# Attention and mixture-of-experts layer on one core: head 0's query rows on another DMA queue

## The reference

```python
xn = _layernorm(x)                                   # (1, 4096, 256)
q = (xn @ Wq.T); k = (xn @ Wk.T); v = (xn @ Wv.T)    # 16 heads of 16
energy = einsum('bqhd,bkhd->bhqk', q, k)
attn = softmax(energy / sqrt(256), axis=-1)
out = einsum('bhqk,bkhd->bqhd', attn, v)
scores = softmax(xf @ gate_w.T); idx = top_k(scores + gate_b, 2)
y = sum over the 2 chosen experts of weight * (silu((xf@w1+b1)*(xf@w3+b3)) @ w2 + b2)
z = the same expert form with the shared weights
return x + out + y + z
```

## Time and profile before

| | |
|---|---|
| median of 3 runs | 2168.85 us (2167.26 to 2175.11) |
| span of the profiled execution | 2166.9 us |
| PE busy | 2141.9 us, 99% |
| ACT busy | 2019.5 us, 93% |
| DVE busy | 814.3 us, 38% |
| POOL busy | 243.2 us, 11% |
| chain that ended last | PE 91%, ACT 7%, DVE 1% |

### The profile page before, as it was taken

How to read it: one execution, slowest core, us unless ns; L and a number is a source line. 1 busy time by engine, 2 the same in 40 slices (tenths; PEclk the granted TensorE clock), 3 DMA queues, 4 the chain that set the end, 5 groups by cost and what they waited for, 6 DMA issues and landing times.

```text
span 2166.9 us, 38385 instructions
## 1 busy us (share of the span) xinstructions
PE 2141.9 (99%) x15772; PEld 977.0 (45%) x15772; DVE 814.3 (38%) x1541; ACT 2019.5 (93%) x2229; POOL 243.2 (11%) x242
## 2 busy tenths in 40 slices
PE   8899999999999999999999999999999999999998
PEld 5732344444444444444444444444444444444322
DVE  7531234334434434434334334334334434544200
ACT  6599999999999999999999999999999999999998
POOL 0102665200000000000000000000000002223200
PEclk9999999999999999999999999999999999999999
DMA  8661434222222213213222322213213222332120
GB/s 286 241 226 47 133 107 132 75 63 66 74 66 68 78 51 83 77 51 85 63 62 71 79 62 73 79 49 85 71 55 85 63 74 72 104 99 64 57 79 3
DMA packets 225758, 187.27 MB, mean 86 GB/s; under 512 B 112407, under 2 KB 194926, under 8 KB 225582
## 3 DMA queue, kind: packets, MB, share of 16 engines
q1 hardware_dynamic: 212702, 149.35, 24.1%
q0 software_dynamic: 11824, 35.40, 5.1%
q10 hardware_dynamic: 1056, 0.07, 0.0%
HBM read 130.21 MB, written 54.53 MB: 85 GB/s over the span
## 4 chain that ended last, share of the span: by engine, by line
PE 91%; ACT 7%; DVE 1%; DMA 0%; issue 0%; SPq 0%; DVEq 0%; ACTq 0%
PE PS L842 41%; PE PS L829 29%; PE PS L854 12%; ACT probs L1112 6%; PE PS L865 6%; PE PS L664 0%; PE PS L665 0%; PE PS L668 0%; DMA qk_parts<-probs 0%; DVE probs L1248 0%; DVE stats L1224 0%; PE PS L640 0%; ACT x_parts L997 0%; ACT x_full L998 0%; PE PS L731 0%
## 5 line engine op out<-in xcount | busy, mean ns | idle before, releaser
L1112 ACT ACTIVATE probs<-PS 128x1024 f32<-128x1024 f32 x2048 | 1920.0, 1081 | 94.9 <-PE PS L829 80.1
L842 PE MATMUL PS<-probs,v_head 128*32 128x512 f32 x8192 | 1001.1, 601 | 1.0 <-ACT probs L1112 0.8
L829 PE MATMUL PS<-q_ring,k_stack 50*128 50x512 f32 x4096 | 741.3, 446 | 5.2 <-ACT probs L1112 3.5
L829 PEld LDWEIGHTS PS<-q_ring,k_stack 50*128 50x128 f32 x4096 | 332.8, 185 | 623.5 <-ACT probs L1112 564.2
L842 PEld LDWEIGHTS PS<-probs,v_head 128*32 128x32 f32 x8192 | 206.6, 108 | 447.2 <-issue 361.2
L1508 DVE TENSOR_SCALAR gate_in<-PS,bias_sb 128x256 f32<-128x256 f32 x165 | 79.6, 482 | 754.5 <-PE PS L854 735.7
L854 PE MATMUL PS<-x_hi,w_hi 128*128 128x256 f32 (+1 forms) x660 | 201.6, 305 | 0.0
L854 PE MATMUL PS<-x_hi,w_lo 128*128 128x256 f32 (+1 forms) x660 | 186.5, 283 | 0.0
L854 PE MATMUL PS<-x_lo,w_hi 128*128 128x256 f32 (+1 forms) x660 | 185.5, 281 | 0.0
L1172 POOL DMA_DIRECT2D slot_y<-y_sb x39 | 27.8, 714 | 1320.7 <-DVE y_sb L1576 1287.1
L854 PEld LDWEIGHTS PS<-x_hi,w_hi 128*128 128x128 f32 (+1 forms) x660 | 118.6, 180 | 60.1 <-issue 60.1
(11 more groups left out here) (166 smaller groups left out, 1194.4 us busy)
## 6 DMA issues: line engine op xcount, KB each, us to landing
w_raw<-in_w SPq DMA_DIRECT2D x110, 352.0 KB
k_stack<-qk_parts SPq DMA_DIRECT2D x120, 128.0 KB
w_raw<-in_w SPq DMA_DIRECT2D x55, 256.0 KB
q_ring<-qk_parts SPq DMA_DIRECT2D x384, 32.0 KB
slot_x<-part_a SPq DMA_DIRECT2D x39, 256.0 KB, 2.3
slot_in<-slot_x SPq DMA_DIRECT2D x156, 64.0 KB, 2.4
slot_y<-y_sb POOLq DMA_DIRECT2D x39, 256.0 KB, 2.6
qk_parts<-part_a SPq DMA_DIRECT2D x18, 512.0 KB, 4.0
```

The source lines that it names most:

```text
L829: last = pe.matmul(bank(2 * score_buffer(turn, g) + r), k_stack[rows, kt * P:(kt + 1) * P], q_ring[rows, sweep, i * QC:(i + 1) * QC], star ...
L842: last = pe.matmul(bank(O_BANK)[VW * j:VW * (j + 1), :], v_head[:, kt, :], probs[:, slot, (j % 2) * QC:(j % 2 + 1) * QC], start=(kt == 0), ...
L1112: nc.scalar.activation(probs[:, prob_slot(g), :], bank(2 * score_buffer(h, g), 2), ACT.Exp, scale=ENERGY_SCALE).then_inc(s_exp, 1)
```

## The change

Six edits:

- `load_q_rows`, `load_q_shift` and `store_shift` take the queue as an argument. Head 0's first sweep (12 row loads, the store of the shift's first half, 4 shift loads) is issued by GpSimd, on a semaphore of its own, `s_qfirst`. SP goes from key chunk 6 straight to query chunk 4. The shift's second half stays on SP, behind chunk 7.
- Query chunks 4 to 7 each get a store semaphore (`s_qlate`). `keep_values(12)` waits for chunk 4's alone.
- Query chunk 6 stands in `key_part[1]` instead of `probs`; ACT therefore waits for the store of key chunk 7 before it splits chunk 6.
- The shift's semaphore becomes two, one for each half.
- GpSimd's memset of `w2_raw` and of `zeros` stand behind its new DMAs, with waits for chunks 5 and 6. DVE's router waits for chunks 6 and 7.
- ACT gets one exponential of one element, behind the last square root.

```diff
-        query_part = [in_values, in_stage, in_values, in_stage, in_values, in_stage, in_xn, key_part[0]]
+        query_part = [in_values, in_stage, in_values, in_stage, in_values, in_stage, key_part[1], key_part[0]]
@@ store_queries
-                    sp.dma_start(store_v[s][:, 0:DT, c * QC:(c + 1) * QC], query_part[c][:, s, :, :].bitcast(f32)).then_inc(s_qst[c % 2], 16)
+                    landed = s_qst[c % 2] if c < FIRST else s_qlate[c - FIRST]
+                    sp.dma_start(store_v[s][:, 0:DT, c * QC:(c + 1) * QC], query_part[c][:, s, :, :].bitcast(f32)).then_inc(landed, 16)
@@ SP
-            for half in range(2):
-                sp.wait_ge(s_qst[half], stored(FIRST - 2 + half))
-            load_q_rows(0, 0)
             store_queries(4)
             store_queries(5)
             sp.wait_ge(s_kst[(NCH - 1) % 2], stored(NCH - 1))
             load_k_chunk(NCH - 1)
-            store_shift(0)
             store_queries(6)
             store_queries(7)
-            sp.wait_ge(s_sst, 16 * NP_)
-            load_q_shift(0, 0, s_q[0])
+            store_shift(sp, 1)
             sp.wait_ge(s_flag, 1)
             flag = sp.value_load(flag_i[0:1, 0:1], min_val=0, max_val=1)
-            store_shift(1)
-            for half in range(2):
-                sp.wait_ge(s_qst[half], stored(NCH - 2 + half))
+            for c in range(FIRST, NCH):
+                sp.wait_ge(s_qlate[c - FIRST], 16 * NP_)
@@ PE, scores
-                    pe.wait_ge(s_q[sweep], h * HEAD_Q + HEAD_Q)
+                    if h == 0 and sweep == 0:
+                        pe.wait_ge(s_qfirst, HEAD_Q)
+                    else:
+                        pe.wait_ge(s_q[sweep], (h + sweep) * HEAD_Q)
@@ ACT
                 if i == 0 and c == 6:
-                    act.wait_ge(s_tr, NCH)
+                    act.wait_ge(s_kst[1], stored(7))
                 if n == 12:
-                    act.wait_ge(s_qst[0], stored(6))
+                    act.wait_ge(s_qlate[0], 16 * NP_)
             nc.scalar.activation(qnorm[HALF:P, :], bank(5)[HALF:P, :], ACT.Sqrt).then_inc(s_qn, 1)
+            nc.scalar.activation(rec[0:1, 0:1], ident_sb[0:1, 0:1], ACT.Exp)
@@ POOL
-            pool.wait_ge(s_kst[1], stored(NCH - 1))
-            pool.wait_ge(s_qst[1], stored(NCH - 1))
+            for half in range(2):
+                pool.wait_ge(s_qst[half], stored(FIRST - 2 + half))
+            load_q_rows(nc.gpsimd, 0, 0, s_qfirst)
+            store_shift(nc.gpsimd, 0)
+            pool.wait_ge(s_sst[0], 16 * NP_)
+            load_q_shift(nc.gpsimd, 0, 0, s_qfirst)
+            pool.wait_ge(s_qlate[1], 16 * NP_)
             nc.gpsimd.memset(w2_raw[FT[2]:P, 2, :], 0.0).then_inc(s_wz, 1)
             pool.wait_ge(s_wz, 1)
             pool.wait_ge(s_v, NT // 2)
+            pool.wait_ge(s_qlate[2], 16 * NP_)
             nc.gpsimd.memset(zeros, 0.0).then_inc(s_zero, 1)
```

More of the change, by code:

```diff
@@ L271, in layer_program @@
         s_qst = [sem("s_qst0"), sem("s_qst1")]
+        s_qlate = [sem(f"s_qlate{i}") for i in range(NCH - FIRST)]
         s_wh = sem("s_wh")
@@ L380, in f_half, with load_q_rows, load_q_shift, store_shift @@
             return PS[:, F_BANK * QC + w * CH:F_BANK * QC + (w + 1) * CH]
+        q_cols = qk_parts.rearrange("s p (w c i r n) -> s p w c i r n", w=2, c=QCH, i=2, r=2)
+        shift_cols = qshift_parts.rearrange("s h (w c i r n) -> s h w c i r n", w=2, c=QCH, i=2, r=2)
+        def load_q_rows(queue, h, sweep, landed):
+            for r in range(2):
+                for i in range(2):
+                    dst = q_ring[r * HALF:r * HALF + ROWS, sweep, i * QC:(i + 1) * QC].bitcast(f32)
+                    for s in range(2):
+                        queue.dma_start(dst[s * HD:(s + 1) * HD], q_cols[s, ds(h * HD, HD), sweep, :, i, r, :]).then_inc(landed, 16)
+                    queue.dma_start(dst[SHIFT + NP_:ROWS], q_cols[0, ds(h * HD, HD), sweep, :, i, r, :]).then_inc(landed, 16)
+        def load_q_shift(queue, h, sweep, landed):
+            for r in range(2):
+                for i in range(2):
+                    dst = q_ring[r * HALF + SHIFT:r * HALF + SHIFT + NP_, sweep, i * QC:(i + 1) * QC].bitcast(f32)
+                    queue.dma_start(dst, shift_cols[:, ds(h, 1), sweep, :, i, r, :].rearrange("s h c n -> (s h) c n")).then_inc(landed, 16)
+        def store_shift(queue, half):
+            rows = slice(half * HALF, (half + 1) * HALF)
+            cols = slice(half * T // 2, (half + 1) * T // 2)
+            for s in range(NP_):
+                queue.wait_ge(s_s1, NP_ * half + s + 1)
+                queue.dma_start(qshift_parts[s, :, cols].rearrange("h (c t) -> c h t", c=FIRST), spart[rows, s, :].bitcast(f32)).then_inc(s_sst[half], 16)
         block = ctx.enter_context(nc.Block())
@@ L454, in store_queries @@
                     sp.wait_ge(ready, query_job(c) + DT)
-                    sp.dma_start(store_v[s][:, 0:DT, c * QC:(c + 1) * QC], query_part[c][:, s, :, :].bitcast(f32)).then_inc(s_qst[c % 2], 16)
-            def store_shift(half):
-                rows = slice(half * HALF, (half + 1) * HALF)
-                cols = slice(half * T // 2, (half + 1) * T // 2)
-                for s in range(NP_):
-                    sp.wait_ge(s_s1, NP_ * half + s + 1)
-                    sp.dma_start(qshift_parts[s, :, cols].rearrange("h (c t) -> c h t", c=FIRST), spart[rows, s, :].bitcast(f32)).then_inc(s_sst, 16)
+                    landed = s_qst[c % 2] if c < FIRST else s_qlate[c - FIRST]
+                    sp.dma_start(store_v[s][:, 0:DT, c * QC:(c + 1) * QC], query_part[c][:, s, :, :].bitcast(f32)).then_inc(landed, 16)
             for c in range(NCH):
@@ L1105, in _ @@
                     if h == 0 and g == 6:
-                        act.wait_ge(s_sst, 32 * NP_)
+                        for half in range(2):
+                            act.wait_ge(s_sst[half], 16 * NP_)
                     if h == 0 and g == 8:
@@ L1369, in _ @@
                 dve.wait_ge(s_kst[1], stored(NCH - 1))
-                for half in range(2):
-                    dve.wait_ge(s_qst[half], stored(NCH - 2 + half))
+                for c in range(FIRST, NCH):
+                    dve.wait_ge(s_qlate[c - FIRST], 16 * NP_)
                 V.memset(q_every[SHIFT:SHIFT + NP_, :].bitcast(f32), 0.0).then_inc(s_qzero, 1)
@@ L1384, in _ @@
                         dve.wait_ge(s_loop, h * NT + t + 1)
-                dve.wait_ge(s_sst, 32 * NP_)
+                for half in range(2):
+                    dve.wait_ge(s_sst[half], 16 * NP_)
                 dve.wait_ge(s_gt, 1)
@@ L1413, in _ @@
             dve.wait_ge(s_kst[1], stored(NCH - 1))
-            dve.wait_ge(s_qst[1], stored(NCH - 1))
+            for c in (6, 7):
+                dve.wait_ge(s_qlate[c - FIRST], 16 * NP_)
             link(V.reduce_max(rs[:, 0, :], lg, axis=AX))
```

37 lines of the change are left out of this document (12 added, 25 removed).

## The result

The changed kernel takes 2161.48 us (median of 5 runs, 2159.6 to 2164.43) against 2168.85 (also 5 runs by then, 2167.26 to 2175.11): a ratio of 0.9966, interval 0.9955 to 0.9977, or 7.4 us less. That is within 0.5% of no change, inside the range, 1.8 us above the number forecast. The profiled execution, of 2162.4 us, is the longest of the five (the others have spans of 2157.6 to 2161.3), so a reader of its rows sees a poor case; how poor, the experiments tell. A run's time is in nearly all runs 1.7 to 2.1 us above its span (2164.43 against 2162.4 here). The 1.95 us between the span and the median before is that difference and no sign of an execution faster than the median. The two profiled executions are 4.5 us apart, so their rows show 4.5 us of the gain, not 7.4.

What follows compares the result with a forecast made beforehand. The chain of waits over PE and ACT, delayed before the first exponential, was taken as the bound. The terms -7.44, -0.73 and -0.97 sum to -9.14 us, from 2168.85 to 2159.7 us; range (8 in 10) 2155.0 to 2166.0.

Steps and rivals of the forecast that it cites:

- Pair 12's wait: Value copies before the attention: waiting for chunk 4's store alone removes ACT's 9.29 us idle time; -7.44 us.
- scores start at 102.43: Start of attention on PE: all values there at 102.37, so first scores at 102.43 against 109.87.
- The price of head 0's rows on POOL: Head 0's loads: twelve at 0.82 us; shift loads land 100.5 to 103.2, needed at 102.43; no cost taken.
- The table load: Before ACT's first exponential: the 1.28 us load moves behind the square root into idle time; -0.73 us.
- The clock: First exponentials: PE at 2.4 GHz instead of 1.2, so no stall before the sixth; -0.97 us.
- PE has only its 0.70 us gap ahead of the scores: Start of attention: PE idles 0.70 us instead of 5.89, so its clock was expected to stay at 2.4 GHz.
- Chunk 6's buffer: ACT's copy of chunk 6 waits for key chunk 7's stores: cost 0 to 0.5 us, taken as 0.
- Shift rows late: Rival: slow POOL issue delays head 0's scores; 2167 to 2169, or 2163 partly; 2161.5 to 2168 given 0.22.
- POOL held up: Rival: POOL takes 2.08 us a DMA, first exponential near 123.7; slower than before, 2181 us; chance 0.04.
- A clock dip elsewhere: Rival: head 1's 1.83 us stall goes, 2157.9 or 2156.5, or a new one comes, 2161.5; dips gone 0.15.
- the border I drew between them: 2161.5 us: forecast as summed within 2158 to 2161.5 (0.57), shift rows partly or wholly late 2161.5 to 2168 (0.22).

Runs made afterwards that it cites:

- the control: The changed kernel again with no edit, 10 runs: 2160.49 us, ratio 0.9974 to the kernel before.
- experiment 7: Changed kernel with chunk 5's store held until the shift rows are written, in two comparisons: 2158.0 us (0.9963) and 2157.97 us (0.9967).
- Experiment 8: Changed kernel with the stores of query chunks 5, 6 and 7 held until the first half's shift store has landed: 2157.89 us, ratio 0.9964.
- experiment 10: The kernel of experiment 7 with each 128 KB shift store issued as two of 64 KB, outer dimension halved: 2162.08 us, ratio 0.9975.
- Experiment 1: Changed kernel with head 0's row loads, the first half's shift store and the shift loads back on SP: 2164.68 us, ratio 0.9996.
- experiment 3: Changed kernel without the single dummy exponential: 2158.56 us, ratio 0.9963.
- experiment 4: Changed kernel with head 0's first shift rows read from long-stored query rows, that sweep's real shift left out: 2157.1 us, ratio 0.9958.
- Experiment 2: Changed kernel with the finer semaphore undone, so pair 12 waits for chunk 6's store as well: 2160.96 us, ratio 0.9982.
- Experiment 9: Changed kernel with the shift store on SP behind chunk 5, plus 24 unread matmuls before the scores: 2158.31 us, ratio 0.9971 (without them 0.9978).

## Why the prediction came out as it did

**Pair 12's wait (-7.44): right in mechanism, 1.9 us too large in the profiled execution.** The wait is gone and the values run through, the last copy at 102.57 against 102.37 forecast. From there the step "scores start at 102.43" failed: they started at 104.34, -5.53 instead of -7.44. At the sixth exponential, behind which the sum was to be complete, the profiled execution leads by 6.05 us (110.63 against 116.68) of the 9.14. In the control and in experiment 7 they lagged the last copy by 0.3 to 0.7 us more than the 0.70 us that the kernel before shows.

**The price of head 0's rows on POOL: two terms wrong, with opposite signs.** Issuing was put at 0.82 us a DMA and took 0.51 for a row load and 0.55 for a shift load, so the twelve were over at 84.6, not 87.4. That gain is lost at once, since the shift rows are only ready near 88. Landing was put at 4.1 to 6.8 us for the shift store and 4.1 for the loads; the store's was 8.6, and 6.5 to 8.7 in the other executions with it on POOL, and the last load's 4.2 to 5.9. This is the mis-sized term. Both figures were borrowed from DMAs of another kind, of 256 and 512 KB; a bound of 8.7 would have put the loads' landing at 105.1 and their lateness at 2.7 us (an estimate by the prediction's own sum). I also wrote that SP's later DMAs move ahead by 5.7 us and asked only whether they would be in time, not what they would stand beside: the DMA share from 84 to 92 us rose from 0.39 to 1.03. Experiment 8 shows that this is not the main part: with SyncE's stores held the store's second DMA still took 7.6 us, within the scatter of the kernels that hold nothing. Why 256 KB keep under two of sixteen engines busy there stays open; experiment 10 shows only that smaller pieces with a smaller outer dimension are no faster.

By the fit in the Trainium skill (DMA: Bandwidth & Descriptors, Anatomy of one DMA — SWDGE (gpsimd) path) the loads would have landed at 96.6, an estimate from its figures; the trace has 104.2. The same page of the Trainium skill says (Issuing engines are not separate DMA queues) that another issuer saves only the issue time, which is usually small beside the DMA. Experiment 1 shows more at stake: on the old queue the shift loads stand behind the late chunks' stores and go out at 102.83 instead of 97.51, and the whole gain is gone.

**The table load (-0.73): right, but not additive.** Experiments 3 and 4 give 0.73. In the profiled execution the rows were later than the load would have been, so by the estimate under experiment 3 the term was worth nothing.

**The clock (-0.97): right in mechanism, wrong for the profiled execution.** The step "PE has only its 0.70 us gap ahead of the scores" failed. With idle times of 0.70 (experiments 3, 4 and 8), 1.00, 1.01 and 1.38 the clock stayed and no sixth exponential stalled. With 2.41 (after), 2.46, 3.24, 3.67 and 6.68 it fell, and the stalls were 1.07, 0.85, 1.53, 0.62 and 2.42. (Experiment 2 has its long wait, 3.33 us, ahead of the last value pair; the clock fell there too, and the stall was 1.43.) The stalls do not grow with the wait. Experiment 9 turns it round with work in the gap.

**Chunk 6's buffer (0): right.** Key chunk 7's stores did land later (7.5 us), but ACT's copy of chunk 6 was not delayed.

**The rivals.** *Shift rows late* is what the profiled execution shows, by the landing and not by POOL's issue cost as I had built it; the control lies nearer to the forecast. That the number is only 1.8 us off is in part luck: the four loads were issued in 2.20 us instead of 3.3, which hides 1.1 us of the longer landing. The outcome varies between the two from execution to execution, and the median of 2161.5 lies on the border I drew between them. *POOL held up* didn't occur: none of the 18 DMAs took over 0.71 us. *A clock dip elsewhere* matters more than I allowed. Experiment 1 shows no dip at 250 or 2020 us, though its start is that of the kernel before, and has a span of 2162.9 instead of 2166.9. The profiled executions of experiments 1, 9 and the second one of experiment 7 have a clock of 1.00 from 240 to 260 us, all others 0.83 to 0.88 in one 10 us half of it, and none of the edits is in that place. I took the profiled execution's dips for part of the kernel, yet the same kernel had medians of 2165 to 2166.5 in the later comparisons. So the gain is 7.4 us in the first comparison and 5.6 in the second by the ratio of 0.9974 (5.0 by the medians), and both intervals hold 6.

## What to carry to other kernels

When a wait is removed, price the chain that then ends last from rows of its own kind, or make the range as wide as the lack of such rows asks; here a 128 KB store was priced from others of 256 and 512 KB and was up to 1.9 us above the bound. Look too at the traffic that the change itself creates, though here it cost less than it seemed. A store followed by a load of the same bytes cost its two landings (6.5 to 8.7 and 4.2 to 5.9 us here), no shorter in pieces or from SyncE's queue, so it has to start early or go. Where TensorE waited 2.4 us or more ahead of the scores the wait cost twice, and where it waited 1.4 us or less it did not; throw-away matmuls in the gap kept the second part.

## What was not expected of the hardware

GpSimd issued plain loads of 4 and 32 KB in 0.51 to 0.70 us and stores of 128 KB in 0.63 to 0.67, below its 256 KB ones and not far from SyncE, which takes 0.36 to 0.43 for the same 32 KB load in a quiet stretch. Of the two 128 KB stores, issued 0.75 us apart on GpSimd, the first landed after 3.0 to 5.6 us and the second after 6.5 to 8.7, 7.6 even with the 16 engines busy for only 0.16 of their time between 92 and 96 us (experiment 8), while 512 KB stores landed after 2.8 to 3.8: size did not order them. And the control ran between 2155.99 and 2162.5 us: its two shortest executions have mean granted clocks of 0.999 and 1.000, its three longest 0.996 to 0.997. In these ten runs the time goes with TensorE's clock.
